# Cross-attention context: one ScalarE read of each transposed bank, rounding on VectorE, low parts shared by VectorE and GpSimd

## The reference, cut to what matters

```python
x = _layernorm(tgt, ln1_g, ln1_b)                    # tgt: 8 x 224 x 512
...                                                  # causal self-attention, 16 heads of 32
result = tgt + sa_out
xq = _layernorm(result, ln2_g, ln2_b)
xs = _layernorm(src, ln2_g, ln2_b)                   # src: 8 x 750 x 512, the context
kv = xs @ ed_wkv
k2, v2 = (_heads(t) for t in jnp.split(kv, 2, axis=-1))
q2 = _heads(xq @ ed_wq)
wei2 = jnp.einsum('bhtd,bhjd->bhtj', q2, k2) * scale
wei2 = jax.nn.softmax(wei2, axis=-1)
ed_out = _merge(jnp.einsum('bhtj,bhjd->bhtd', wei2, v2)) @ ed_wproj + ed_bproj
result = result + ed_out
...                                                  # feed-forward on the same tgt, added too
```

## Time and profile before

| what | value |
|---|---|
| median of 3 runs | 1369.85 us |
| lowest and highest run | 1369.48 and 1372.99 us |
| span of the profiled execution | 1372.2 us |
| the run nearest above that span, taken as the profiled execution's own time | 1372.99 us |
| granted TensorE clock, mean | 0.984 |
| PE busy | 1310.9 us (96%) |
| DVE, ACT, POOL busy | 794.4, 662.1, 701.5 us |

### The profile page before, as it was taken

The page is one execution under the profiler, slowest core; times in us unless marked ns, Lnnn a source line. Parts: engine busy times, 40 slices in busy tenths (PEclk is TensorE's granted clock), DMA queues, the critical chain, the costliest instruction groups (busy, mean ns, idle before and its releaser), DMA issues.

```text
span 1372.2 us, 24578 instructions
## 1 busy us (share of the span) xinstructions
PE 1310.9 (96%) x9193; PEld 1082.5 (79%) x9193; DVE 794.4 (58%) x2007; ACT 662.1 (48%) x1609; POOL 701.5 (51%) x577
## 2 busy tenths in 40 slices
PE   7999999999899999998788999999999999999997
PEld 6888888888788888887677787878877787887874
DVE  6613223232777777776655575756757566575565
ACT  5311111232666665666433656474665647456444
POOL 3232221322444555556733767666676766667661
PEclk9999999999999999999599999999999999999999
DMA  7400102114647776547267685777677587766641
GB/s 237 145 18 16 62 31 77 46 60 117 139 86 178 166 186 148 122 123 185 63 142 119 100 128 98 132 123 125 101 127 120 101 137 104 142 101 112 90 71 41
DMA packets 100400, 151.67 MB, mean 111 GB/s; under 512 B 10197, under 2 KB 63229, under 8 KB 99514
## 3 DMA queue, kind: packets, MB, share of 16 engines
q1 hardware_dynamic: 100282, 150.11, 53.8%
HBM read 66.74 MB, written 24.12 MB: 66 GB/s over the span
## 4 chain that ended last, share of the span: by engine, by line
PE 76%; POOL 8%; issue 5%; DVE 5%; DMA 3%; ACT 2%; SPq 1%; POOLq 0%; ACTq 0%; DVEq 0%
PE ps L1727 18%; PE ps L453 11%; PE ps L164 10%; PE ps L423 10%; PE ps_pair L1744 6%; PE ps L1759 5%; PE ps L1773 5%; PE ps L1832 3%; POOL ca_partial L1586 2%; DMA ca_k_stack<-ca_keys 2%; POOL ca_xT L1473 1%; DMA sa_K_stack<-sa_rows 1%; PE ps L1207 1%; PE ps L1791 1%; PE ps L1227 1%
## 5 line engine op out<-in xcount | busy, mean ns | idle before, releaser
L1664 DVE TENSOR_REDUCE ca_maxes<-ps 112x1 f32<-112x375 f32 x512 | 256.5, 541 | 106.0 <-PE ps L1759 103.9
L1607 ACT ACTIVATE ca_probT<-ps_pair 125x448 f32<-125x448 f32 x384 | 210.3, 554 | 181.5 <-PE ps_pair L1744 179.6
L1586 POOL TENSOR_TENSOR ca_partial<-ca_partial,ca_probT 125x896 f32<-125x896 f32 x118 | 249.2, 2112 | 93.6 <-ACT ca_probT L1607 89.0
L312 POOL TENSOR_TENSOR ff_hT<-ff_hrelu,ff_hT 128x512 fp32r<-128x512 f32 (+1 forms) x64 | 77.9, 1218 | 203.2 <-DVE ff_hT L394 203.2
L1759 PE MATMUL ps<-ca_k_stack,ca_q_stack 96*112 96x376 f32 x512 | 168.7, 352 | 6.9 <-issue 3.6
L1744 PEld LDWEIGHTS ps_pair<-ca_q_stack,ca_k_stack 98*125 98x125 f32 x768 | 130.2, 186 | 44.0 <-issue 31.9
L1744 PE MATMUL ps_pair<-ca_q_stack,ca_k_stack 98*125 98x224 f32 x768 | 156.2, 285 | 1.3 <-ACT ca_probT L1607 1.2
L423 PE MATMUL ps<-ff_w,ff_hT 128*128 128x512 f32 x672 | 155.5, 390 | 0.0
L1727 PE MATMUL ps<-w_b,ca_xT 128*125 128x512 f32 x576 | 151.2, 398 | 3.1 <-POOL ca_xT L1473 2.5
L1727 PE MATMUL ps<-ca_xT,w_a 128*128 128x376 f32 x768 | 153.1, 335 | 0.0
L423 PEld LDWEIGHTS ps<-ff_w,ff_hT 128*128 128x128 f32 x672 | 125.6, 188 | 25.8
(11 more groups left out here) (145 smaller groups left out, 2433.0 us busy)
## 6 DMA issues: line engine op xcount, KB each, us to landing
ca_k_stack<-ca_keys SPq DMA_DIRECT2D x96, 376.0 KB, 8.0
sa_Q_stack<-sa_rows SPq DMA_DIRECT2D x96, 112.0 KB, 3.5
sa_K_stack<-sa_rows SPq DMA_DIRECT2D x96, 112.0 KB, 3.7
ca_q_stack<-q_out SPq DMA_DIRECT2D x96, 112.0 KB, 9.5
ctx_tokens<-in_ctx_dram SPq DMA_DIRECT2D x14, 672.0 KB
ctx_tokens<-in_L_xattn_ff_w_dram SPq DMA_DIRECT2D x16, 512.0 KB, 4.4
q_out<-sa_yT SPq DMA_DIRECT2D x16, 448.0 KB, 3.7
wp_lo<-wp_out SPq DMA_DIRECT2D x6, 1024.0 KB, 4.8
```

Source lines behind the costliest of these rows:

```text
L312: pool.tensor_tensor(hT[:, LO, m % RING, 0:width(g)], hrelu[i % 2][:, 0:width(g)], hT[:, HI, m % RING, 0:width(g)].bitcast(F32), ALU.subtr ...
L1586: pool.tensor_tensor(total, total, half(a), ALU.add).then_inc(partial_done, 1)
L1607: act.activation(probT[u // GH][0:JT, u % GH].rearrange("p a t -> p (a t)"), ps_p[u % 2][0:JT, 0:2 * T], ACT.Exp).then_inc(exp_done, 1)
L1664: dve.tensor_reduce(maxes[:, q, j, a:a + 1], ps_s[n % 3][0:TQ, 0:JH], AX_X, ALU.max).then_inc(s_read, 1)
```

## The change

ACT reads each transposed bank once, into the float32 copy, and releases it. The rounding to the high part moves to DVE, which copies `xT_f32` to `xT[:, HI]` within SBUF (L1719 of the changed kernel) as the first part of `T_rest`. The low part follows: for the first half of the tokens (and all of batch 0) on DVE, right behind its own rounding; for the second half of batches 1 to 7 on POOL, which now waits for DVE's rounding (`xhi_done`). The counter of finished low parts becomes two, one for each half.

```diff
     def context_low(eng, b, m, a):
 
-        wait_acc_read(eng, "T", b, m, a)
+        eng.wait_ge(xhi_done, XT * b + KT * a + m + 1)
         eng.tensor_tensor(xT[:, LO, m, a, 0:JH], xT_f32[:, m, a, 0:JH],
-                          xT[:, HI, m, a, 0:JH].bitcast(F32), ALU.subtract).then_inc(xlo_done, 1)
+                          xT[:, HI, m, a, 0:JH].bitcast(F32), ALU.subtract).then_inc(xlo_done[a], 1)
+
+    def low_by_pool(b, m, a):
+
+        return b > 0 and a == 1
...
-        if name == "T_rest" and item[1] > 0:
+        if name == "T_rest" and low_by_pool(*item[1:]):
             context_low(pool, *item[1:])
...
-            act.activation(xT[:, HI, m, a, 0:JH], acc[:, 0:JH], ACT.Identity,
-                           bias=cn["columns"][:, 3 * KT + m:3 * KT + m + 1],
-                           scale=cn["columns"][:, 2 * KT + m:2 * KT + m + 1]).then_inc(xhi_done, 1)
             act.activation(xT_f32[:, m, a, 0:JH], acc[:, 0:JH], ACT.Identity,
                            bias=cn["columns"][:, 3 * KT + m:3 * KT + m + 1],
                            scale=cn["columns"][:, 2 * KT + m:2 * KT + m + 1]).then_inc(acc_read(*product), 1)
...
-        if name == "T_rest" and item[1] == 0:
-            context_low(dve, *item[1:])
+        if name == "T_rest":
+            _, b, m, a = item
+            wait_acc_read(dve, "T", b, m, a)
+            dve.tensor_copy(xT[:, HI, m, a, 0:JH], xT_f32[:, m, a, 0:JH]).then_inc(xhi_done, 1)
+            if not low_by_pool(b, m, a):
+                context_low(dve, b, m, a)
...
-                pe.wait_ge(xlo_done, XT * b + XT // 2 * (a + 1))
+                pe.wait_ge(xlo_done[a], KT * (b + 1))
...
-                pe.wait_ge(xlo_done, XT * b + XT // 2)
+                pe.wait_ge(xlo_done[0], KT * (b + 1))
```

More of the change, by code:

```diff
@@ L1430, in cross_attention @@
     ohi_done, olo_done, wp_lo_landed = sem("ohi_done"), sem("olo_done"), sem("wp_lo_landed")
-    khi_done, mhi_done, xhi_done, xlo_done, shift_done = (
-        sem(n) for n in ("khi_done", "mhi_done", "xhi_done", "xlo_done", "shift_done"))
+    khi_done, mhi_done, xhi_done, shift_done = (sem(n) for n in ("khi_done", "mhi_done", "xhi_done", "shift_done"))
+    xlo_done = [sem(f"xlo_done{a}") for a in range(2)]
     NG = KT * B
```

## The result

The changed kernel takes 1399.68 us (median of 4 runs, 1398.62 to 1401.40), the kernel before 1370.72 us (4 runs, 1369.48 to 1372.99). The ratio is 1.021, with a 95% interval from 1.0194 to 1.0227: 29 us slower. The forecast was 1388 us, with a range from 1364 to 1401. The batches now come 85.3 us apart instead of 80.9. The ratios in this document leave out one slow run, 1814.51 us, of the ten of e3b.

A forecast was written before the change was run, and what follows sets the result against it. PE sets the pace, losing time almost only in the T stretch; with the change it waits for DVE. Seven stretches +21 us, batch 0 -1, vanished waits: +18.5, so 1391.5 us profiled, 1388 us median, range 1364 to 1401.

The forecast's parts named there:

- walk step 4: T stretch after PE's stand: DVE paces PE through the remaining scores, so value product V 0 comes 3.0 us later.
- more turns lost: Rival: POOL keeps its turn between additions, or its low parts hold roundings; 4.5 us lost per batch, 1401 us, chance 0.13.
- Steps 1 and 2, the holds: T stretch: POOL's low part holds T1's subtraction; its slot 7 additions hold T2's rounding and subtraction, about 2 us each.
- The odd row length: DVE's roundings of 375 columns: odd but equal on both sides, so expected to be held too; no run showed one.
- the rival with one hold: Rival: the odd-length rounding is not held, only subtractions are; +1.4 us per batch, 1379 us, chance 0.17.
- Step 3, PE's stand: T stretch: score s7b is reduced only at 921.3 us, so PE stands at s9a from about 917.4 until then.
- Step 5: After V 0: POOL's slot 11 pair ends at 931.95 us, before it is needed; the 3.0 us per stretch stand.
- The two waits that vanished: Small waits for POOL's sums that go away, some 0.2 us per batch.
- Batch 0: First batch: fewer ACT reads on the chain against DVE's held subtraction; -1 us, from -2 to +2.
- The prediction's three reads: Batch 0: three second reads by ACT on the chain, 0.55 us each, giving back 1.65 us in all.
- The sum: Whole kernel: +21 us for seven stretches, -1 for batch 0, vanished small waits make it +18.5; 1388 us forecast.
- The gain that was named for an undisturbed DVE: Rival: DVE never held where it matters; -0.45 us per batch, 1366 us, or 1360 if its work fits; shared chance 0.20.

The follow-up runs named there:

- e3b: Kernel before, with POOL's two additions of slot 7 in the seven T stretches cut to 8 of 224 columns: 1370.22 us, ratio 0.9987.
- e3: Changed kernel, with POOL's two additions of slot 7 in the seven T stretches cut to 8 of 224 columns: 1366.61 us, ratio 0.9965.
- e10: Changed kernel with 33 more transposes on PE ahead of score tile s9a in each of the seven T stretches: 1388.98 us, ratio 1.012.
- e9: Kernel before with batch 0 changed, DVE rounding every second T from the bank, and T3's low part ahead of POOL's slot 7 pair: 1375.86 us, ratio 1.0033.
- e6: Kernel before, with batch 0 alone as in the change: 1368.74 us, ratio 0.9979.
- e0: Kernel before, without an edit, timed and profiled once more: 1371.25 us, ratio 0.9994.
- e1: Changed kernel, but POOL makes all low parts of batches 1 to 7 and DVE only rounds there: 1375.50 us, ratio 1.0029.
- e7: Kernel before, ACT still reading twice, but DVE makes the low parts of T0 to T3 in batches 1 to 7: 1373.42 us, ratio 1.0016.

## Why the prediction came out as it did

The direction and the mechanism were right; the loss was too small by 10 us, because **walk step 4 reckoned PE's way from s9a to V 0 at full clock**. The walk's own range, 1383 to 1396 us, missed the 1399.68 us. The stated range took it in only because of the share given to "more turns lost", which is not what happened; that part was luck.

- *Steps 1 and 2, the holds: right.* The pair began 0.47 us before DVE came to T2 (half a microsecond in the walk); T2's subtraction ended 4.64 us after the pair's start (4.8 in the walk); T1's subtraction was held by `D_low` (0.99 us). e3 shows that the pair is the cause. This held in six stretches; in the first, T2's rounding was through before POOL's addition took its turn, and T3's was held in its place.
- *The odd row length: settled.* The roundings of 375 columns are held, 1.83 against 0.34 us, so the condition of the rival with one hold fails. The row that the prediction had for even ones was thin evidence: 0.46 us for 448 columns, where the shortest of that form in the trace of before takes 0.38 us. The Trainium skill's page "VectorE: DVE Perf Modes", section "What auto-detection actually checks", lets a row length that is equal on both sides enter the two-port mode; the rows agree.
- *Step 3, PE's stand: right.* 3.65 us at s9a, in the walk 3.9.
- *Step 4: mis-sized.* From s9a to V 0 the walk gave 4.65 us; the changed kernel took 6.31, and e10, with the same holds and PE kept at work, 4.70. T0 to V 0 grew by 2.94 us in e10, where the prediction had 3.0, and by 4.55 in the changed kernel. The missing term is the clock: 1.6 us per batch.
- *Step 5: right.* V 0 to D is 6.92 us, so nothing more is lost. The two waits that vanished are worth 7.02 - 6.92 and 61.67 - 61.59 us, together the 0.2 us of the sum. That what is won up to V 0 is passed on whole holds only while POOL's sums are in time: e9 won 0.87 us and gave back 1.83.
- *Batch 0: mis-sized the other way.* -1 us was forecast; the timed difference is -2.9 us (e6; -4.4 to -1.4 by its interval). The prediction's three reads are those of the first profile's chain; that of e0 has four, and the normalisation that should have taken time back is not on e6's chain.
- *The sum.* From the first V 0 to the last, seven batches, the changed kernel takes 580.80 us and e0 549.56: +31.2. e10 takes 569.98: +20.4, where the prediction had 21 - 1.5 = 19.5. So 10.8 us are the clock's, and with about -4 ahead of the first V 0 in these executions the spans differ by 27.0. The profiled execution of before was taken for one of 1373.0 us; with 2.5 us outside the span, as in the changed kernel's, it was nearer to 1374.7, an estimate. The forecast, set against the median, does not hang on it.
- *The rivals.* "More turns lost" had the right time, 1401 us, by a wrong road: DVE did get its turn between the two additions, and the roundings of T4 to T7 took 0.72 us at most. The gain that was named for an undisturbed DVE, 0.45 us per batch, is 0.57 in e3 (0.34 against e3b, which has the cut too).

## What to carry to other kernels

Before work is moved onto an engine, look for what another engine does at that minute: 0.9 us of VectorE work became 4.1 us because GpSimd's additions had begun half a microsecond earlier (in one stretch, with a lead of 0.30 us, the first operation was not held at all), while the same rounding read from PSUM took 0.66 us beside them. When a walk makes TensorE stand for microseconds in a dense stretch, price the return at the lower clock too. And when a wait is taken away, follow the queue that it covered to its next deadline: here it was GpSimd's second pair of additions, 7 us behind the place that was mended, and the best versions found, one read for batch 0 alone (0.9979) and every second rounding from the bank (0.9980, with that same change for batch 0 in it), win 0.2%.

Not tried: the pair of slot 11 ahead of POOL's low parts of T4 to T6, which would give D its sums earlier.

## What the runs showed of the hardware that was not expected

The granted clock fell to the 1.2 GHz level during each of the six 3.65-us stands at s9a (from 836.4, 921.8, 1007.1, 1092.4, 1177.8 and 1263.1 us, 6.8 us each), in a stage where PE is otherwise busy for 99% of the time; with transposes in the stand (e10) it never fell there. In the first stretch, with stands of 1.73 and 1.61 us, it fell for 3.4 us from 757.9 us on. Shorter stands in the other kernels did not tell so clearly: with about 1.5 us at V 0 (e1) it fell for 3.4 us in five of seven batches, with 1.00 us at s9a (e7) in one, with 1.76 us at D (e9) in none. Where it fell in e1, V 0 to D took 8.48 to 8.56 us, otherwise 7.38: 1.1 to 1.2 us for 3.4 us at half clock.
